# A graph layer's sums kept turned, with GpSimd's odd-step sums and shifts interleaved tile by tile

## What is computed

```
msg  = edge_weight[:, None] * layernorm(x)[dst]
aggr = segment_sum(msg, src)
aggr = aggr + (1 + eps) * layernorm(x)
h    = relu(relu(aggr @ W1 + b1) @ W2 + b2)
x1   = x + (h - mean(h)) * scale * rsqrt(var(h)) + offset
out  = x1 + top-2 mixture of 8 experts on layernorm(x1)
```

## Time and profile before

| | us |
|---|---|
| median of 3 runs | 1289.24 |
| lowest, highest | 1284.93, 1290.47 |
| the profiled execution, its own time | 1288.74 |
| its span, first to last instruction | 1286.8 |
| outside the span | 1.9 |

### The profile page before, as it was taken

The page is one execution under the profiler, slowest core; times in us unless marked ns, Lnnn a source line. Parts: engine busy times, 40 slices in busy tenths (PEclk is TensorE's granted clock), DMA queues, the critical chain, the costliest instruction groups (busy, mean ns, idle before and its releaser), DMA issues.

```text
span 1286.8 us, 25490 instructions
## 1 busy us (share of the span) xinstructions
PE 901.3 (70%) x6921; PEld 615.4 (48%) x6922; DVE 733.5 (57%) x1645; ACT 677.3 (53%) x2181; POOL 670.6 (52%) x678
## 2 busy tenths in 40 slices
PE   2383487548765476564677767686279999999995
PEld 1131232225332233232465645575167778787883
DVE  4664286548655474454564564887835555555553
ACT  7894398219873178752233332463245555555552
POOL 3836356752676626666457647322434544544542
PEclk9985599669776688865676678796589999999998
DMA  4114222332233313333244432173012223223222
GB/s 121 61 47 140 58 62 87 95 84 69 83 90 95 92 38 94 89 103 112 62 131 148 124 119 92 54 212 130 2 58 40 43 48 49 45 45 49 46 45 25
DMA packets 59608, 102.47 MB, mean 80 GB/s; under 512 B 10298, under 2 KB 43048, under 8 KB 59400
## 3 DMA queue, kind: packets, MB, share of 16 engines
q0 software_dynamic: 29520, 65.96, 21.1%
q1 hardware_dynamic: 30008, 35.55, 8.7%
HBM read 84.27 MB, written 17.20 MB: 79 GB/s over the span
## 4 chain that ended last, share of the span: by engine, by line
PE 42%; DVE 16%; ACT 11%; issue 10%; another core or an unknown queue 6%; DMA 2%; DVEq 2%; POOL 1%; POOLq 0%; ACTq 0%
PE bank L999 7%; ACT Wall L1085 7%; PE bank L985 4%; PE bank L987 4%; PE bank L986 4%; ACT RB L1093 4%; PE bank L843 3%; PE bank L1001 3%; PE bank L841 3%; DVE RA L1564 3%; PE bank L854 3%; PE bank L842 2%; DVE Wall L1564 2%; PE bank L806 2%
## 5 line engine op out<-in xcount | busy, mean ns | idle before, releaser
L675 POOL DMA_INDIRECT Wall<-xl_d,gbuf x391 | 392.4, 1004 | 292.1 <-PE bank L843 137.6
L1093 ACT ACTIVATE RB<-RB,gbuf 128x128 f16<-128x128 f16 x488 | 178.9, 424 | 301.9 <-DVE RB L1551 208.7
L841 PE MATMUL bank<-Wall,RB 128*128 x488 | 167.7, 344 | 155.6 <-DVE Wall L1564 54.4
L1085 ACT ACTIVATE Wall<-Wall 128x128 f32<-128x128 f16 (+1 forms) x782 | 246.9, 383 | 24.8 <-DVE Wall L1482 16.8
L1564 DVE TENSOR_TENSOR RA<-RA,bank 128x256 f32 x244 | 102.0, 418 | 269.3 <-remote 143.2
L1205 ACT ACTIVATE RA<-bank,b1T 128x128 f32<-128x128 f32 x448 | 128.1, 369 | 120.9 <-PE bank L987 120.8
L734 POOL DMA_INDIRECT out_dram<-RA,slot_tok x56 | 101.1, 1805 | 160.8 <-ACT RA L1211 143.0
L806 PE MATMUL bank<-Wall 128*128 128x512 f16 (+1 forms) x391 | 154.7, 444 | 33.9 <-ACT Wall L1085 20.8
L985 PE MATMUL bank<-RA,Wall 128*128 128x128 f16 x896 | 175.4, 221 | 0.3 <-issue 0.3
L987 PE MATMUL bank<-RA,Wall 128*128 128x128 f16 x896 | 175.4, 221 | 0.0
L986 PE MATMUL bank<-RA,Wall 128*128 128x128 f16 x896 | 175.3, 221 | 0.0
(11 more groups left out here) (314 smaller groups left out, 1584.3 us busy)
## 6 DMA issues: line engine op xcount, KB each, us to landing
stage<-in_L_ffn_W SPq DMA_DIRECT2D x10, 1024.0 KB
Wall<-xl_d,gbuf POOLq DMA_INDIRECT x391
Wall<-in_L_ffn_W SPq DMA_DIRECT2D x6, 1024.0 KB, 6.6
Wall<-in_x SPq DMA_DIRECT2D x4, 640.0 KB, 6.7
xl_d<-Wall SPq DMA_DIRECT2D x4, 640.0 KB
out_dram<-RB SPq DMA_DIRECT2D x4, 640.0 KB
xn_d<-RA SPq DMA_DIRECT2D x4, 640.0 KB
RB<-in_x SPq DMA_DIRECT2D x1, 1792.0 KB
```

Of the source, the lines that this page charges most:

```text
L675: pool.indirect_dma_start(out=ring[:, t % RING * 2 * D:(t % RING + 1) * 2 * D], out_offset=None, in_=xl_d, in_offset=bass.IndirectOffsetOn ...
L841: mm(o, high, ring[:, bass.ds(at, D)], start=True, stop=False)
L1085: last = act.activation(hi_word[:, n % SR, k * S:(k + 1) * S], hi_hot[:, n // HB % 2, n % HB // 2, 0:S, n % 2], ACT.Copy, scale=pay[k][:, ...
L1093: act.activation(low, high, ACT.Copy, scale=rec_r[:, n:n + 1]).then_inc(sw_built, 1)
```

## The change

Four things are done.

1. **The sums are kept turned.** In `agg_step` the gathered rows become the stationary operand and `Sw` the moving one: for each half of the features (kc = 0, 1) three products of 128 columns, six in all for three of 256 before. The sums `acc` and `acc_odd` then hold features along the partitions, and the product with W1 takes them as they are. The transposes L907 and the copies L1148 go; W1 is scaled by `w_back` once instead (`gw1_scaled`, one ACT instruction).
2. **The start of the odd sums** has to be turned too: in the first sort TensorE turns the normalised rows, tiles in pairs behind sort steps 33, 36 and so on to 69 (`turn_rows`, 100 products with an identity in fp16), and DVE writes them times (1 + eps) to `acc_odd` (`own_sums`, 12 instructions of 512 columns and one of 256) at its sort steps 40, 48, 56, 64 and 72. The five instructions L1539 go. `acc_set` is counted in 13 pairs.
3. **GpSimd's order in stage 3.** The sum of tile t waits until the first product of tile t - 6 is done (AHEAD = 6), each is followed by the shift of one tile (t - 6), and the normalised rows come in fives between them.
4. **The second product** uses two banks in turn, so that its wait for ACT's relu is one tile looser, and three of the late weight conversions wait for the sums of their own tiles, not of all.

```diff
@@ agg_step
-                mm(o, high, ring[:, bass.ds(at, D)], start=True, stop=False)
-                mm(o, low, ring[:, bass.ds(at, D)], start=False, stop=False)
-                mm(o, high, ring[:, bass.ds(at + D, D)], start=False, stop=True).then_inc(agg_mm, 1)
+                for kc in range(KC):
+                    o = agg_out(n)[:, kc * P:(kc + 1) * P]
+                    row_high, row_low = (weights(at, RING_AT + k * D + kc * P, P) for k in range(2))
+                    mm(o, row_high, high, start=True, stop=False)
+                    mm(o, row_high, low, start=False, stop=False)
+                    m = mm(o, row_low, high, start=False, stop=True)
+                m.then_inc(agg_mm, 1)
@@ TensorE, first sort
+            def turn_rows(p):
+                tiles = range(2 * p, min(2 * p + 2, NT))
+                pe.wait_ge(xl_done, tiles[-1] + 1)
+                if p >= 3:
+                    pe.wait_ge(acc_set, p - 2)
+                for k, t in enumerate(tiles):
+                    for kc in range(KC):
+                        o = own_out(p)[:, (k * KC + kc) * P:(k * KC + kc + 1) * P]
+                        mm(o, x_parts[:, t, kc * P:(kc + 1) * P], ident_h[:, :], start=True, stop=False)
+                        m = mm(o, x_parts[:, t, D + kc * P:D + (kc + 1) * P], ident_h[:, :], start=False, stop=True)
+                m.then_inc(x_turned, 1)
@@ DVE
-            for g in range(NT // G):
-                rows = slice(G * g, G * (g + 1))
-                dve.tensor_scalar(x_in[:, rows, :], x_in[:, rows, :], eps1[:, 0:1], None, ALU.mult).then_inc(acc_set, 1)
+            def own_sums(n):
+                for p in range(PAIRS):
+                    if n - HB <= turned_behind(p) < n:
+                        if p == 0:
+                            dve.wait_ge(eps_ready, 1)
+                        dve.wait_ge(x_turned, p + 1)
+                        o = own_out(p)
+                        at = 2 * p * D
+                        dve.tensor_scalar(acc_odd[:, at:at + o.shape[1]], o, eps1[:, 0:1], None, ALU.mult).then_inc(acc_set, 1)
@@ GpSimd, stage 3
-            for t in range(NT):
-                pool.tensor_tensor(acc[:, t, :], acc[:, t, :], acc_odd[:, t * D:(t + 1) * D], ALU.add).then_inc(acc_sum, 1)
-                if t >= 2 * G - 1 and (t + 1) % G == 0:
+            for t in range(NT + 4 * G):
+                u = t - AHEAD
+                if 0 <= u < NT:
+                    pool.wait_ge(h1_mm, u + 1)
+                if t < NT:
+                    pool.tensor_tensor(acc[:, t, :], acc[:, t, :], acc_odd[:, t * D:(t + 1) * D], ALU.add).then_inc(acc_sum, 1)
+                if u == XEARLY:
+                    pool.wait_ge(x_late, 32)
+                if 0 <= u < NT:
+                    pool.tensor_tensor(x1[:, u, :], x1[:, u, :], gof_bc, ALU.add).then_inc(x_shift, 1)
+                g = (t - 3 * G + 2) // G - 1
+                if (t - 3 * G + 2) % G == 0 and 0 <= g < NT // G:
+                    pool.wait_ge(xn_coef, g + 1)
+                    for v in range(G * g, G * (g + 1)):
@@ TensorE, stage 3
-                    for kc in range(KC):
-                        m = nc.tensor.transpose(bank[t % 2][:, kc * P:kc * P + P], acc[:, t, kc * P:kc * P + P], ident[:, :])
-                    m.then_inc(t_mm, 1)
-                                   aggT[t % 2][:, kc * P:kc * P + P], start=kc == 0, stop=kc == KC - 1)
+                                   acc[:, t, kc * P:kc * P + P], start=kc == 0, stop=kc == KC - 1)
-                    if t >= 1:
-                        pe.wait_ge(h2_relu, t)
+                    if t >= 2:
+                        pe.wait_ge(h2_relu, t - 1)
@@ ACT, stage 3
+            act.wait_ge(mlp_in, 80)
+            act.activation(gw1, gw1, ACT.Copy, scale=w_back[:, 0:1]).then_inc(gw1_scaled, 1)
-                    act.activation(aggT[t % 2], bank[t % 2][:, 0:D], ACT.Copy, scale=w_back[:, 0:1]).then_inc(t_out, 1)
```

More of the change, by code:

```diff
@@ L430, in agg_out, with own_out, h2_out @@
             return bank[1 + n // 2 % 3][:, n % 2 * D:(n % 2 + 1) * D]
+        def own_out(p):
+            return bank[1 + p % 3][:, 0:min(2, NT - 2 * p) * D]
+        def h2_out(t):
+            return bank[4 * (t % 2)][:, 0:D]
+        PAIRS = (NT + 1) // 2
+        turned_behind = lambda p: 33 + 3 * p
         def groups(c):
@@ L526, in _ @@
             sp.wait_ge(xl_stored, 16 * (NT // G + 1))
[L527 removed]
+            sp.wait_ge(acc_set, PAIRS)
             sp.dma_start(gw1, gW1.rearrange("(c p) n -> p c n", p=P)).then_inc(mlp_in, 16)
@@ L876, in _ @@
                     rank_part(1, i - HB)
+                if p < PAIRS and turned_behind(p) == i:
+                    turn_rows(p)
+                    p += 1
+            assert p == PAIRS
             pe.wait_ge(bias_mm, 2)
@@ L1169, in _ @@
                     act.wait_ge(h2_mm, t + 1)
-                    act.activation(h2[:, t, :], bank[4][:, 0:D], ACT.Relu).then_inc(h2_relu, 1)
+                    act.activation(h2[:, t, :], h2_out(t), ACT.Relu).then_inc(h2_relu, 1)
                 if n in LATE_AT:
@@ L1531, in _ @@
                     rank_part(1, n - HB)
+                if n % HB == 0 and n > turned_behind(0):
+                    own_sums(n)
             records(0)
@@ L1587, in _ @@
             dve.wait_ge(acc_zeroed, 1)
-            dve.wait_ge(acc_set, NT // G)
+            dve.wait_ge(acc_set, PAIRS)
             dve.wait_ge(xl_stored, 16 * (NT // G + 1))
```

59 lines of the change are left out of this document (20 added, 39 removed).

## The result

The changed kernel takes 1302.42 us (median of 4 runs, 1301.89 to 1308.81) beside 1287.09 us for the kernel before (median of 4 runs, 1282.24 to 1290.47). The ratio is 1.0132, with a 95% interval of 1.0096 to 1.0168: it is slower by 12 to 22 us. The forecast was 1285 with a range of 1272 to 1316, "same" as the likeliest.

What follows compares the result with a forecast made beforehand. Stage 2 was taken as bound by a gather-step-update loop, stage 3 by GpSimd's run holding DVE, then DVE. 1288.7 + 0 + 4 - 13.6 + 6.2 = 1285.3, forecast 1285 us, range 1272 to 1316.

Steps and rivals of the forecast that it cites:

- same: Whole kernel: a time neither below 1282.8 us nor above 1295.7, chance 0.36.
- What bounds the kernel: Stage 2: a loop of gather, landing, TensorE's step and update; stage 3: GpSimd's unbroken run holding DVE, then DVE.
- The 2.1 us between two products: Stage 2: two neighbouring TensorE products start 2.1 us apart, no cause shown; cited for a price by the instruction.
- Part 1, the turned start: First sort: DVE's added reads mostly hidden; first gather 2.0 us later, first step 2.2 earlier; taken 0, ends -2 and +4.
- Part 2, six products: Stage 2: six products take 0.6 us, half of a gather's 1.25; taken +4 us, ends -10 and +32.
- Rival B: Stage 2: the loop pays for TensorE's instructions, 32 us instead of 4, total 1313 us; chance 0.22.
- the slope between two stretches: Stage 2: 1.4 more products per us came with 0.05 us a gather, 32 us if all is TensorE's instructions.
- B's place: Where TensorE's instructions would cost: stage 2 between gathers, deciding from about 1.49 us a gather on.
- Part 3, to the first moments: Stage 3 start: first product 1.3 us earlier, four tiles save 0.9, L1384's wait falls by 11.4; together -13.6 us.
- Part 4, the later pairs: Stage 3: GpSimd's later sums and shifts hold DVE up by half, less existing waits; +6.2 us, ends 0 and +16.4.
- Rival C: Stage 3: each GpSimd pair holds DVE up in full, 16.4 us for 6.2, total 1295 us; chance 0.14.
- Slower: Whole kernel: a time above 1295.7 us, chance 0.31.

Runs made afterwards that it cites:

- e3: Changed kernel without turning the odd sums' start, the five old L1539 instructions back in place (for timing only): 1.0097 of the kernel before.
- f3: Changed kernel with gathers 8 to 31 held back and the odd sums' start left unturned: 0.9934 of the kernel before.
- f2: Kernel before with GpSimd's new stage 3 order and gathers 8 to 31 held back, measured again: 0.9743 of the kernel before.
- e7: Kernel before with GpSimd's new stage 3 order and gathers 8 to 31 held back, sums not turned: 0.9804 of the kernel before, 1260.3 us.
- e2: Kernel before with each step's three products cut into two of 128 columns, edge weights still stationary: 1.0243 of the kernel before.
- e9: Kernel before with three more one-column products ahead of each step's three, their output overwritten: 1.0185 of the kernel before.
- e1: Kernel before with only GpSimd's new stage 3 order and looser late waits, sums not turned: 0.9933 of the kernel before, 1284.5 us.
- e8: Changed kernel with GpSimd's old stage 3 order, all sums, shifts of five tiles, no waits between: 1.0216 of the kernel before.
- e5: Kernel before with each of gathers 8 to 31 waiting for the step eight earlier: 0.9878 of the kernel before.
- f4: Kernel before with new GpSimd order, gathers 8 to 31 held back and some shifts moved ahead of stage 2's last sum: 0.9775 of the kernel before.
- e6: Changed kernel with each of gathers 8 to 31 waiting for the step eight earlier: 0.9973 of the kernel before.
- e12: Kernel before with one more one-column product a step, on a chip where before takes 1157 to 1158 us: 1.0048 of the kernel before.
- g2: Kernel before with only GpSimd's new stage 3 order, on a chip where before takes 1157 to 1158 us: 0.9929 of the kernel before.

## Why the prediction was wrong

**What bounds the kernel** was read rightly for stage 3 and half for stage 2: the loop of gather, step and update, and the late updates, were seen in the earlier trace rows, but what one more product costs in that loop was given hardly any weight. The 2.1 us between two products that the prediction pointed at the earlier trace rows don't explain it by themselves: such stalls grew from 5 to 47, but 38 of the 47 lie in the middles of the chunks, which hold 3.5 of the 17.1 us.

**Part 1, the turned start: forecast 0, ends -2 and +4; measured +6.8 in the trace.** The step that failed is "the others fall where the batch is a little early; I take them as hidden". The price of a read was right: 2.06 us for three, 0.69 each. So was the cost of the first three reads (up to 2.0 forecast, 2.2 measured), and the last five were hidden as forecast. But the five in between cost 1.8 and 3.3 us: DVE had 0.49 and 0.69 us to spare a batch, and three reads are 2.06. I compared with the wait behind the last batch (3.68 us) and not with that behind each. Even the upper end was too low, because it gave the five at most 2 us. DVE's own wait for TensorE ahead of the last batch also grew, from 0.69 to 2.05 us, so the delay is passed on through TensorE and ACT. That the reads are the cause rests on e3 and f3: without them the first gather is back at 104.0 and 103.5 us. How much of it reaches the end is shown on kind B only, nearly all. The gain on the other side, 2.2 us for the first step, vanished with it: the first step's product starts 6.0 us later (115.6 for 109.6).

**Part 2, six products: forecast +4, ends -10 and +32; measured +17.1 in the trace, 17 to 25 us by f3 against f2 and e7.** This term is the miss, and the step that failed is its size. Rival B's claim that TensorE's instructions are paid for was right on kind A (e2: +2.4%, e9: +1.9%), and its price of 32 us was near e2's 31 (0.08 times 391 is 31.3; the text rounds up). How the loop comes to pay is not explained by it. The value was taken at an eighth of the upper end, because the slope between two stretches could have another cause; e9, in which nothing but added products is new, shows that these alone cost 19.1 us of stage 2. B's place, "between gathers", is neither confirmed nor refuted: the middles of the chunks cost 3.5 of 17.3 us in the changed kernel, but 12.6 of 29 in e2 and 9.2 of 11.7 in f3 against f2. The 0.10 us a product from the experts spoke for no change only because GpSimd's pace of 1.25 us a gather was taken for the bound everywhere; behind the last gather it isn't, and six products cost 3.2 us there. e9's three extra products cost 24 us / 1464 = 16 ns each on average, which sounds like nothing beside 0.10 and is 2% of the kernel.

**Part 3, to the first moments: forecast -13.6; measured -14.4** (19.6 instead of 34.1 us behind stage 2). L1384's successor took 0.17 us, less than one pair. e1 and e8 show it from both sides: the order alone gives 11.9 of it, and the turned sums alone 0.0, since the small sum then waits 16.05 us.

**Part 4, the later pairs: forecast +6.2, ends 0 and +16.4; measured +4.2** (74.8 instead of 70.6). The term was right in kind and 2 us too large. DVE's scaling with two SBUF inputs (L1682) took 0.83 to 0.95 us in the first group instead of 0.48, so it lost 0.35 to 0.47 us beside a pair, less than the 0.65 that half of a pair is. Rival C, the whole pair each time, is out. The Trainium skill's rule (SBUF — State Buffer, "Who interferes with whom": the second of the two to issue blocks until the first is done) agrees with the trace for a single instruction (0.35 to 0.47 us lost beside single ones of 0.72 us), and 16.05 us in e8 repeat that a run queued without a gap counts as one instruction.

**The sum.** By the terms of the trace: +6.8 + 17.1 - 14.4 + 4.2, and 0.3 in the rest of stage 3, make +14.0. Parts 3 and 4 together were forecast at -7.4 and came to -9.9 with that rest. Parts 1 and 2 were forecast at +4 and came to +23.9. "Slower" had a chance of 0.31, B alone 0.22; with the products' price counted at the measured slope instead of at an eighth of it, it would have been the forecast. B's own sign came true: stage 2 over 690 us, where 675 within 5 was forecast. That its price fits is in part luck: the same products cost 4 to 6 us on kind B. The measured 1302 lies inside the range of 1272 to 1316, but the forecast change was a gain of about 2 us and the measured one a loss of 15.

**What stays open.** Why TensorE's updates and products are held up on kind A and not on B is not known. If chip number 7 of the record is one chip, it was of both kinds within half an hour, and the kind is no fixed property of a chip; no run here tests what sets it. Many of the stalls are near multiples of 0.7 us. They are something else than the late updates, since the kernels with three products and the first ring held back have updates as late as the others (median 3.1 to 3.8 us in e5, e7, f2 and f4) and at most one stall each. Nor is it shown how six products come to cost 17 to 25 us on kind A, since stalls and lost time don't lie in the same places, nor whether it is the number of products a step or of all TensorE's instructions together.

## To carry to other kernels

Before work is added "beside" a wait, compare it with the wait in each turn of the loop, not with the longest one at its end. In a loop in which engines wait for each other a product of TensorE has a price beside its columns: three more in each of 488 steps, of one column each, cost 24 us on kind A, and one more 5.6 us on kind B; turning an operand by cutting products in two must win more than that. And where GpSimd's unbroken run holds up an instruction of DVE with two SBUF inputs (12.76 to 16.05 us for a sum of five columns here), GpSimd is best made to pause: the order alone, without the turned sums, is 0.7% faster, and with the first ring of gathers held back 2 to 2.6% on kind A and 0.6% on kind B.

## What the runs showed of the hardware

- On kind A updates of TensorE's products reach DVE late all through the stage with indirect gathers: 3.1 to 3.9 us in the median where DVE was waiting, in each of fourteen traces, and 0.13 to 0.14 us in each of six on kind B. The longest lie in the first ring, where GpSimd issues 32 gathers without a wait: DVE's waits of 10.96 and 15.92 us before, 37.02 and 37.64 us in two executions of the changed kernel. With GpSimd held back there the longest wait of the ring is 6.00 us (e5) and 8.79 us (e6).
- On kind A TensorE's products also start late, many by about 0.7 or 1.4 us, inside a step, without any wait in the program: 0 to 5 times with three products a step, 31 to 47 times with six. On kind B it happens once in six traces (e12), and not with six products.
- The kernel before takes 1287 to 1294 us on one kind and 1157 to 1158 on the other. By e1 and g2, one kernel on both, 132 of 134 us lie in stage 2. A change in such a stage is best timed on both: this one is 1.3% slower on A and 0.35% on B.
